# Attention side work in smaller pieces on other engines, and the scores of the next pair issued later on TensorE

## The reference

```python
x = x + 0.5 * ffn(layernorm(x))     # 8 experts in 4 groups of 2, top group by router, both experts of it
x = x + attn(layernorm(x))          # sliding windows: W = 128, stride 64, 7 windows per row of 512
x = x + 0.5 * ffn(layernorm(x))     # same weights again

# attention, for each of the 8 batches, 16 heads of 16 columns, 7 windows:
scores = q_win @ k_win.T / 4 + pos_bias[head]
out_win = softmax(scores) @ v_win
ctx[window] += out_win               # overlapping windows are added, then divided by their count
return ctx @ Wo + bo
```

## Time and profile before

| what | us |
|---|---|
| median of 3 runs (lowest, highest) | 1549.4 (1544.67, 1550.34) |
| the profiled execution, its own time | 1547.95 |
| its span, first to last instruction | 1546.2 |
| PE busy / PEld / DVE / ACT / POOL in the span | 1303.2 / 845.9 / 918.6 / 646.2 / 244.2 |
| first scores of batch 0, of batch 1, of batch 7 | 524.1 / 589.6 / 1081.0 |
| first output projection of batch 7 behind the loop | 1167.0 |

### The profile page before, as it was taken

The page is one execution under the profiler, slowest core; times in us unless marked ns, Lnnn a source line. Parts: engine busy times, 40 slices in busy tenths (PEclk is TensorE's granted clock), DMA queues, the critical chain, the costliest instruction groups (busy, mean ns, idle before and its releaser), DMA issues.

```text
span 1546.2 us, 33371 instructions
## 1 busy us (share of the span) xinstructions
PE 1303.2 (84%) x8771; PEld 845.9 (55%) x8772; DVE 918.6 (59%) x3765; ACT 646.2 (42%) x2339; POOL 244.2 (16%) x286
## 2 busy tenths in 40 slices
PE   4422699999996798989999899989893799999996
PEld 4411466666664455555565555555563466666664
DVE  5789444444443577777687877787864344444442
ACT  1114322223222476657466575757750122232221
POOL 3322001100011101120111212021212011000100
PEclk9999999999998699888779897989956899999998
DMA  9500442000002101010100202020106121000000
GB/s 303 207 28 28 175 151 59 17 14 14 14 15 80 45 15 49 1 49 15 35 31 9 56 9 57 1 63 2 49 15 248 52 59 55 14 14 14 15 15 14
DMA packets 51247, 81.37 MB, mean 53 GB/s; under 512 B 6912, under 2 KB 34816, under 8 KB 51136
## 3 DMA queue, kind: packets, MB, share of 16 engines
q1 hardware_dynamic: 44320, 61.29, 12.5%
q0 software_dynamic: 6816, 18.81, 3.4%
HBM read 45.81 MB, written 27.97 MB: 48 GB/s over the span
## 4 chain that ended last, share of the span: by engine, by line
PE 61%; DVE 15%; issue 8%; ACT 4%; POOL 2%; DMA 1%; DVEq 1%; SPq 1%; ACTq 0%; POOLq 0%
PE bank L807 24%; PE bank L759 9%; PE bank L825 9%; PE bank L940 6%; DVE w_all L1387 5%; PE bank L896 4%; PE bank L967 3%; DVE w_all L1397 2%; PE bank L978 2%; PE bank L923 2%; DVE hb L1226 2%; ACT sl L637 2%; ACT w_all L719 1%; PE bank L773 1%; DVE stats L1095 1%
## 5 line engine op out<-in xcount | busy, mean ns | idle before, releaser
L719 ACT ACTIVATE w_all<-w_all 128x128 f32<-128x128 f32 x896 | 347.1, 391 | 162.9 <-DVE w_all L1387 161.7
L807 PE MATMUL bank<-w_all,xt 128*128 x1680 | 390.2, 383 | 12.6 <-DVE xt L1238 3.5
L807 PEld LDWEIGHTS bank<-w_all,xt 128*128 128x128 f16 x1680 | 165.1, 98 | 197.0 <-issue 37.1
L1226 DVE SCALAR_TENSOR_TENSOR hb<-bank,ew,sl 128x512 f32<-128x512 f32 x140 | 105.2, 751 | 211.0 <-ACT sl L637 211.0
L1387 DVE CUSTOM_DVE_ANT_0 w_all<-bank,w_all 128x128 f32<-128x128 f32 x896 | 198.2, 286 | 44.7 <-PE bank L940 32.3
L825 PE MATMUL bank<-w_all,ht 128*128 x1680 | 206.2, 273 | 1.2 <-DVE yt L1251 1.2
L637 ACT ACTIVATE sl<-bank,back 128x512 f32<-128x512 f32 x140 | 95.9, 685 | 239.0 <-PE bank L807 239.0
L759 PE MATMUL bank<-ident,w_all 128*128 128x128 f32 x896 | 166.1, 316 | 22.1 <-ACT w_all L719 12.9
L1397 DVE COPY w_all<-bank 128x512 f32<-128x512 f32 x224 | 153.1, 685 | 43.3 <-PE bank L967 43.3
L825 PEld LDWEIGHTS bank<-w_all,ht 128*128 128x128 f16 x1680 | 164.2, 98 | 19.3 <-issue 1.7
L719 ACT ACTIVATION_READ_ACCUMULATOR w_all<-w_all 128x1 f32 x896 | 169.7, 189 | 0.0
(11 more groups left out here) (168 smaller groups left out, 1603.6 us busy)
## 6 DMA issues: line engine op xcount, KB each, us to landing
big<-sorted_rows SPq DMA_DIRECT2D x70, 130.5 KB, 2.1
saved<-w_all SPq DMA_DIRECT2D x16, 512.0 KB, 2.8
w_all<-saved SPq DMA_DIRECT2D x4, 2048.0 KB, 14.1
w_all<-mid SPq DMA_DIRECT2D x9, 512.0 KB, 3.7
big<-in_L_attn_hidden_states SPq DMA_DIRECT2D x8, 512.0 KB, 4.3
w_all<-in_L_ffn_gate_w SPq DMA_DIRECT2D x8, 512.0 KB, 11.2
w_all<-in_L_ffn_up_w SPq DMA_DIRECT2D x8, 512.0 KB, 10.8
w_all<-in_L_ffn_down_w SPq DMA_DIRECT2D x8, 512.0 KB, 11.3
```

The lines of the kernel that those rows point to most:

```text
L719: a = nc.scalar.activation(prob[:, u % NB, h], sbias[:, u % NB, h], ACT.Exp, bias=nmax[:, u % NB, h:h + 1], scale=-1.0, accum_out=rsum[:, ...
L807: mm = nc.tensor.matmul(bank[2 * e + w][:], xt[:, hx, c, :], flat(gu16[:, bass.ds(g * E + e, 1), w, hw, c, :]), start=(i == 0), stop=(i == ...
L1226: nc.vector.scalar_tensor_tensor(out=hb[:, e], in0=bank[2 * e + 1][:], scalar=ew[:, e:e + 1], in1=sl[:, e], op0=ALU.mult, op1=ALU.mult).th ...
```

## The change

The change makes these edits, all in attention:

- `scores` of the next pair moves on TensorE from the head of the even unit to its end, behind `turn`, `values` and the side work; `factors` moves from u % 4 == 2 to u % 4 == 3.
- The side work gets tables of its own for each engine. Projections go in halves (k0a, k0b and so on), logits in four parts. The prepared batch now needs only v0 ahead of its start; v1, v2 and v3 stand in units 1 to 3 of the batch itself.
- The shift of values is three pairs of transfers a batch, each as soon as its values are there; `values` waits by window.
- POOL takes the small operations of both layer norms, both `xa` (8 POOL instructions a batch), and the rest of `choose` and `find_place` behind `best_groups`.
- ScalarE takes `rexp`. VectorE keeps the statistics (one tile a step), the residual and value copies and 5 small operations of routing.
- The scatter moves on POOL to the end of the batch, behind the last `accumulate`, and SP waits for it directly.

```diff
@@ tables @@
-        SIDE = {2: ("stats0",), ... 13: ("k0", "copy_k0"), 14: ("k1", "r_norm0", "copy_k1"), ...
+        PE_SIDE = {1: ("v1",), 2: ("v2",), 3: ("v3",), 5: ("turn_prep",), 7: ("k0a",), 8: ("k0b",), 9: ("o0",),
+                   10: ("o1",), 11: ("o2",), 12: ("o3",), 13: ("k1a",), 14: ("k1b",), 15: ("q0a",), 16: ("q0b",),
+                   18: ("turn_route",), 20: ("l0",), 21: ("l1",), 22: ("l2",), 23: ("l3",), 24: ("q1a",), 25: ("q1b",),
+                   27: ("v0", "rank")}
+        PE_FIRST = {1: ("v1",), 2: ("v2",), 3: ("v3",), 10: ("turn_prep",), 11: ("k0a",), 12: ("k0b",), 13: ("k1a",),
+                    14: ("k1b",), 15: ("q0a",), 16: ("q0b",), 24: ("q1a",), 25: ("q1b",), 27: ("v0",)}
+        PE_LAST = {1: ("v1",), 2: ("v2",), 3: ("v3",), 9: ("o0",), 10: ("o1",), 11: ("o2",), 12: ("o3",),
+                   18: ("turn_route",), 20: ("l0",), 21: ("l1",), 22: ("l2",), 23: ("l3",), 26: ("rank",)}
+        DVE_SIDE = {2: ("copy_v1",), 4: ("copy_v2", "copy_v3"), 10: ("add0",), 11: ("r_stat0", "add1"), 12: ("add2",),
+                    13: ("r_stat1", "add3"), 14: ("r_stat2", "r_stat3"), 20: ("stat0",), 22: ("stat1",), 24: ("best",),
+                    25: ("stat2",), 26: ("stat3",), 28: ("copy_v0",), 29: ("place",)}
...
@@ TensorE, batch @@
                 for u in range(UNITS):
-                    if u % 2 == 0 and ahead(b, u, last):
-                        b2, u2 = ahead(b, u, last)
-                        scores(b2, par if u2 > u else 1 - par, u2, b * (2 * UNITS) + (2 * u + 4))
                     turn(b, u, first_ and u < 2)
                     if u >= 2:
                         values(b, par, u - 2, first_)
...
-                    if u % NQ == 2:
+                    if u % NQ == 3:
                         if u > NQ:
                             factors(b, par, u // NQ - 1)
...
+                    if u % 2 == 0 and ahead(b, u, last):
+                        b2, u2 = ahead(b, u, last)
+                        scores(b2, par if u2 > u else 1 - par, u2, b * (2 * UNITS) + (2 * u + 4))
@@ POOL @@
+            def norm(k, said, n, st, src, mean, rstd):
+                pool.wait_ge(said, n)
...
+                pool.tensor_tensor(rstd, var, mhalf[:], ALU.pow).then_inc(rstd_ready, 1)
+                pool.wait_ge(rstd_ready, k + 1)
+                pool.wait_ge(xnt_psum, k * DC + OPEN)
+                for t in range(TB):
+                    pool.tensor_scalar(xa[:, t, :], src[:, t, 0:D], mean[:, t:t + 1], rstd[:, t:t + 1],
+                                       ALU.subtract, ALU.mult).then_inc(xa_ready, 1)
...
             def batch(b, par, first_, last):
                 pool.memset(ctxt[par][:], 0.0).then_inc(ctx_zero, 1)
+                if not last:
+                    norm(prep_use(b + 1), stat_ready, b + 1, stats, xb, mean_b[:], ln_t[:, 4, :])
                 if not first_:
                     accumulate(b - 1, 1 - par, NWIN - 1)
                     bias_residual(b - 1)
                 for n in range(NWIN - 1):
                     accumulate(b, par, n)
...
-                    if n == (3 if last else 4) and not first_:
-                        scatter(b + (B - 1), route_use(b - 1), stage, B, scattered[1])
+                    if n == NWIN - 3 and not first_:
+                        step = choose(b + (B - 1), stage)
                 if not first_:
+                    find_place(b + (B - 1), B, step)
+                    scatter(b + (B - 1), route_use(b - 1), stage, B)
@@ ScalarE, copy_values @@
+                nc.scalar.activation(rexp[:], rinv.unsqueeze(2).to_broadcast([P, H, HD]), ACT.Copy,
+                                     scale=inv_count[:, n:n + 1]).then_inc(rexp_ready, 1)
@@ VectorE, inverse @@
-                nc.vector.tensor_scalar(rexp[:], bc(rinv, 2, [P, H, HD]), inv_count[:, n:n + 1], None,
-                                        ALU.mult).then_inc(rexp_ready, 1)
@@ SP @@
             def batch(b, par, first_, last):
+                shift_values(b, par, 0)
+                shift_values(b, par, 1)
+                shift_values(b, par, 2)
                 if not first_:
-                    sp.wait_ge(stage_free, b - 1 + OPEN)
+                    sp.wait_ge(scattered, (b - 1) * (16 * TB) + 16 * TB * B)
                     sp.dma_start(stage[:, :, 0:D], rows_of(b - 1)).then_inc(res_loaded, 16)
```

More of the change, by code:

```diff
@@ L122, in macaron_kernel @@
         stats = sb("stats", [P, TB, 6])
+        stats_r = sb("stats_r", [P, TB, 6])
+        rest = sb("rest", [P, TB, G])
+        minus = sb("minus", [P, TB])
+        pair = sb("pair", [P, TB, 2])
+        pair8 = sb("pair8", [P, TB, 2, E])
         ln_t = sb("ln_t", [P, 6, TB])
@@ L266, in flat @@
             return v.rearrange("p a d -> p (a d)")
[L272 to L304, removed]
@@ new lines, in macaron_kernel, with steps @@
+        DVE_FIRST = {2: ("copy_v1", "stat0"), 3: ("stat1",), 4: ("copy_v2", "copy_v3"), 5: ("stat2",), 6: ("stat3",),
+                     20: ("stat0",), 22: ("stat1",), 24: ("stat2",), 26: ("stat3",), 28: ("copy_v0",)}
+        DVE_LAST = {2: ("copy_v1",), 4: ("copy_v2", "copy_v3"), 10: ("add0",), 11: ("r_stat0", "add1"), 12: ("add2",),
+                    13: ("r_stat1", "add3"), 14: ("r_stat2", "r_stat3"), 24: ("best",), 28: ("place",)}
+        def steps(u, first_, last, side, side_first, side_last):
+            return (side_first if first_ else side_last if last else side).get(u, ())
@@ L603, in _ @@
             accumulate(B - 1, 1, NWIN - 1)
-            power(route_use(B - 1), ln_t[:, 5, :], stage[:, :, C_RSTD])
-            scatter(2 * B - 1, route_use(B - 1), stage, B, scattered[1])
+            power(route_use(B - 1), ln_t[:, 5, :], stage[:, :, C_RSTD], B + 1)
+            scatter(2 * B - 1, route_use(B - 1), stage, B)
             scatter_pads(1)
@@ L727, in batch @@
                             copy_values(b - 1, 1 - par, NWIN - 1)
-                    for s in steps(u - 1, first_, last):
+                    for s in steps(u - 1, first_, last, ACT_SIDE, ACT_FIRST, ACT_LAST):
                         if s == "copy_route":
@@ L767, in turn_batch, with logits @@
                     tr.then_inc(xnt_psum, 1)
-            def logits(r, k, lg, src=xnt):
+            def logits(r, k, lg, src=xnt, tiles_=range(TB)):
                 pe.wait_ge(xnt_ready, k * DC + DC)
-                for t in range(TB):
+                for t in tiles_:
                     for c in range(DC):
@@ L1458, in batch @@
                         if s in ("add0", "add1", "add2", "add3"):
                             add_residual(b - 1, int(s[-1]))
-                        if s == "choose0":
-                            parts = choose(b + (B - 1), stage)
-                        if s in ("choose0", "choose1", "choose2", "choose3"):
-                            step = next(parts)
-                        if s == "place":
-                            find_place(b + (B - 1), B, bank[7], step)
-            for t in range(TB):
-                copy_v(0, 0, t)
+            copy_v(0, 0, 0)
```

329 lines of the change are left out of this document (210 added, 119 removed).

## The result

The changed kernel takes 1616.4 us, median of 4 runs (1612.4 to 1628.1), against 1549.9 in 4 runs of the kernel before: a ratio of 1.044, 95% interval 1.037 to 1.051. It is slower, as forecast, but by 67 us and not by 15, and above the end of the range.

A forecast was written before the change was run, and what follows sets the result against it. TensorE was taken as the bound, losing 7.0 us idle and 23 at half clock a batch. Middle batches -12, batch 0 +15.4, batch 7 +2.5, tail +11, prologue -2 gave +15: 1565 us, range 1528 to 1601.

The forecast's parts named there:

- The main term: Attention pairs: transposes wait for VectorE's copy behind the late scores, 4.80 us a bare pair; middle batch 75.9 against 81.9, -6.0.
- the sum: All of attention: middle batches -12, batch 0 +15.4, batch 7 +2.5, tail +11, prologue -2, together +15 us.
- Where the side work is free: TensorE pairs: odd side work and factors cost nothing, even side work adds its time; middle batch 75.9 us at full clock.
- The clock's price: TensorE at 1.2 GHz: one fall of 10 us a middle batch, 3.0 us; batch 0 +8, batch 7 +7.
- POOL's share: POOL's work at the batch's end: xa 0.6 us each, turn_prep 1.4 us late, +1 us a middle batch.
- rival d: VectorE's bias chain stopped by POOL's xa: +34 us on top, 1597 us; chance 0.05.
- The tail: Behind the last batch, turn of unit 26 to first output projection: 21.4 us against 10.1, +11 us.
- The prologue's -2: Before the first scores: only v0 stands ahead of them, so -2 us.
- Rival (b): Clock as low as now or lower, 22 us a middle batch, POOL 2.5 late: 85.0 a batch, 1601 us; chance 0.15.
- (a): TensorE's clock holds in attention: -19 us, 1530 us, faster; chance 0.24.
- (c): Gains and losses cancel, some 65 us at half clock: 1549 us; chance 0.14.

The follow-up runs named there:

- experiment 1: The changed kernel with scores of the next pair back at the head of the even unit; 1508.5 us, ratio 0.979 to the kernel before.
- experiment 2: The changed kernel with VectorE's copy_pt ahead of biased of the next pair in even units; 1582.3 us, ratio 1.028 to the kernel before.
- experiment 4: The kernel before with only the scores moved late, to the end of the even unit; 1651.3 us, ratio 1.072 to the kernel before.
- experiment 12: The kernel of experiment 10 with scores moved back to the end of the even unit; 1615.9 us, ratio 1.050 to the kernel before.
- experiment 9: The changed kernel with the transposes of units 17, 19 and 21 done three times; 1573.9 us, ratio 1.022 to the kernel before.
- experiment 5: The changed kernel again without any edit, measured and profiled anew; 1619.7 us, ratio 1.049 to the kernel before.
- experiment 10: The changed kernel with scores at the head, prepared xa on VectorE and TensorE's side steps moved to where nothing waits; 1453.9 us, ratio 0.945 to the kernel before.
- experiment 8: The kernel before with only rexp moved from VectorE to ScalarE; 1536.9 us, ratio 0.996 to the kernel before.
- experiment 3: The changed kernel with the four transposes of every odd unit done twice; 1572.4 us, ratio 1.019 to the kernel before.
- experiment 6: The changed kernel with the four xa of the prepared batch back on VectorE; 1638.3 us, ratio 1.060 to the kernel before.

## Why the prediction was right in its direction and wrong in its size

- **The main term, the scores moved: right.** A bare pair lasts 4.80 us in batches 1 to 6, as in the sum, and 4.72 in batches 0 and 7; the wait, its place and its releaser are those named. Experiments 1, 2, 4 and 12 show it from four sides.
- **Where the side work is free: nearly right.** By the pairs that ran at full clock, here and in experiment 9, a middle batch without waits for POOL would be some 77.5 us (estimate) for the 75.9 of the sum. Of these 1.6 us 0.6 are the halves of the projections, with a pitch of 1.06 and not 0.9; the rest is 0.1 to 0.3 in several pairs.
- **Two waits that the sum had not seen.** In batches 2, 4, 6 and 7 of the first profile one pair lasts 6.3 to 6.6 us and not 4.7 to 4.9; over batches 1 to 6 that is 0.8 each. VectorE's first `biased` starts 2.9 to 3.0 us behind the scores and not 1.35, and the profile names no instruction that released it:

```profile
710.47 0.29 DVE L1491 CUSTOM_DVE_ANT_0 w_all<-bank,w_all 128x128 f32<-128x128 f32 x1 [4.08 <-remote]
```

Experiment 5, the same kernel, has 4.9 in that place. In batches 3 and 5 the first pair lasts 7.0 us for 5.0, 0.7 a batch on average, with PE waiting 1.8 to 1.9 us; experiment 10 waits 1.9 and 1.6 us in these two batches, and the kernel before 1.5. What ends these waits is not known.
- **The clock's price, the step that failed.** It said: "I take one fall of 10 us a middle batch: 3.0 us". There are 2.3, of 11.7 us, 27.3 us a batch at half clock. And a us of them costs 0.31 (experiment 9), where I had 0.23 to 0.30. So 8.5 us in place of 3.0, six times: +33. In batch 0 the same step has 47.8 us for 31, and 0.31 for 0.25: +7, more than the 4.9 by which batch 0 is off; at full clock it is 2 us shorter than I had it, 1.1 of them by the bare pair of 4.72. In batch 7 it was right, 25 us for 25. The places were right: of 18 gaps of 1.3 us or more at full clock in batches 1 to 6, 12 have a fall right behind them, and experiment 9 took the falls away by filling them. What was wrong was to count two such gaps close together as one fall, and to think only of those two: the wait for POOL's `xa` has a fall right behind it in each of batches 2 to 6. The size of a fall was nearly right (the kernel before has 13 of 10.5 us in batches 1 to 6, which I had read as 14 of 10), their number was not.
- **POOL's share: right in kind, too small.** "I take 0.6" for an `xa`, with bounds 0.3 and 0.73; it is 1.22, beyond both. `turn_prep` waited 2.3 to 2.7 us, in batches 2 to 6, in the first profile, up to 4.2 in the second, for the 1.4 of the sum. Less the part that was a gap anyway, and less the clock, the pair is 1.75 us longer than in batch 1, 1.5 a batch on average for the +1 of the sum. The Trainium skill, GPSIMD Engine Reference, section Engine selection, calls a one-input operation there roughly line-rate; the same four tiles took VectorE 1.37 us together and POOL 4.9, so the measurement decides against it for this form with two per-partition scalars.
- **VectorE stopped by POOL (rival d): did not happen.** `biased` took 284 to 294 ns in all 896 places, 88 of them beside POOL's `xa`. The prediction puts a long `rexp` into each of batches 1 to 7; in the kernel before they came in batches 1 to 6 only, with 2.03 to 2.39 us.
- **The ends.** The tail came as worked out, 21.7 for 21.4. The prologue's -2 did not come: the first scores start at 524.0 as before. The second expert stage is 6.8 us shorter, of which 5.8 lie between the start of the last scatter to the output and the end of the span: 11.9 us in the kernel before and in experiments 4 and 8, 6.1 in all kernels made from the changed one. It goes with the program, but I had no term for it and tested none.
- **The sum.** Batches 1 to 6 were off by 9.1 us each, 55 in all: 5.5 of the 9.1 the clock, 1.6 the pairs at full clock, 0.8 and 0.7 the two waits without a known cause, and 0.5 POOL. Batch 0 was off by 4.9, batch 7 by 0.3. The pieces are estimates, each from its own rows; that they add up to the 9.1 is no proof of each. Rival (b) was the nearest: 22 us of half clock a batch and POOL 2.5 late. It came to 85.0 a batch, with a price of the half clock that was right and an amount that was 5 us too small. Rivals (a) and (c) needed at most 65 us at half clock in the whole stage; there are 240.

## What to carry to other kernels

Before an instruction moves later on a busy engine, write down the loop that its result goes round and compare its length with the work left to cover it: here 3.86 us against 2.0, known before the run and right to 2% (3.78 in the pair shown). Then look at what TensorE's clock makes of the gaps: taking 3.1 us of idle time out of a batch made it 8.0 shorter, so a kernel can win by useless work in a gap (experiment 3) and wins most when the last short waits go (experiment 10). Work given to another engine is late or in time by its place in that engine's queue, not by its duration: `xa` on the fast engine at the wrong place was worse than on the slow one with the scores late (1.060 for 1.049) and no better with the scores at the head, and with TensorE's steps moved to where nothing waits it made the best kernel.

## What the runs showed of the hardware that I had not expected

- POOL takes 1.22 us for a 128x256 fp32 `tensor_scalar` with two scalars per partition, VectorE 0.41, and 0.32 from start to start in a row. POOL's power on 128x4 elements takes 1.04, and small operations in a chain of waits start 0.38 us apart.
- `rexp` on ScalarE takes 502 to 511 ns in all 56 places, 506 to 507 in the 5 beside POOL's `xa`. None of them ran beside POOL's bias addition, where VectorE took up to 2391 ns for it; one of experiment 8 did and took 503.
- The same kernel is faster with more matmuls in it: 336 more in batches 1 to 6, 22 us less.
- A gap of 1.3 us or more did not always bring the clock down: 6 of the 18 in the changed kernel did not, nor did two of 1.6 and 1.9 us in experiment 10, whose batches are otherwise almost without idle time. And falls came without a wait right ahead of them. Experiment 6 has less idle time than the changed kernel and 13 us a batch more at half clock. What decides between these the runs don't settle.
